# The mixer by pairs of sequences inside the first attention, with its short convolution's taps on ScalarE and VectorE

## The chip, the cores and the metric

The kernel runs on one core of a Trainium2 chip. The metric is the device time of one execution in microseconds (us). TensorE (PE in the rows) multiplies matrices, VectorE (DVE), ScalarE (ACT) and GpSimd (POOL) work on tiles of 128 partitions, and SyncE (SP) issues most DMAs. Each engine takes its own instructions strictly in order and waits on semaphores that the others raise.

## The reference

One decoder layer on 16 sequences of 128 tokens with 128 channels. The first stage, the mixer, is all that the change rewrites:

```python
x = jnp.einsum('bld,de->ble', u, W_in) + b_in          # 128 -> 3 * 128 channels
uc = dw_causal_conv(x, short_w, short_b)               # depthwise, 3 taps
q, k, v = uc[:, :D], uc[:, D:2 * D], uc[:, 2 * D:]
v = dw_causal_conv(k * v, inner_w, inner_b)            # depthwise, 4 taps
y = einsum('bld,de->ble', q * v, W_out) + b_out
x = layernorm(x_in + y)
```

Then come a self attention and a cross attention (16 heads of 64, each followed by a residual sum and a layer norm), a feed forward of width 512, and a last stage with 16 experts. The inputs are fp32; projections are made from a high and a low fp32r part of each factor, in three products (`mm_split`).

## The kernel before

`build` calls four things in a row: the allocations, `setup_and_mixer`, `attentions`, `feed_forward`. Each of the last three is a block of its own, so no engine starts on the attentions before all of them have left the mixer.

**The mixer** (`setup_and_mixer`, L162 to L497) works on groups of four sequences (512 columns), in ticks. The short convolution is folded into the weights: VectorE multiplies `w_in` with `tap_rows` (L379), ScalarE and VectorE split the result (L271, L382), and TensorE sums three shifted products for each of the three thirds of the channels (L476 to L478, nine products of 512 columns each). ScalarE adds the bias (L285), GpSimd corrects the first two columns (L333) and forms `KV` (L337), VectorE makes the inner convolution (L408, L412), GpSimd the gate (L342), TensorE the output product (L486), VectorE the residual and its statistics (L419 to L429), GpSimd the power (L353), ScalarE the normalised `N1` (L294), TensorE its transposes (L494), ScalarE and VectorE the parts of `x1T` (L300, L438), and GpSimd two sums for later residuals (L362). The same ticks split the six attention weights and the context (L306, L449, L313, L455) out of a ring of four raw tiles.

**The attentions** (`attentions`) are a software pipeline over 32 items, an item being one sequence in one of the two attentions. Iteration p of the loop does, on every engine, some part of items p-4 to p+1, in an order that is written out by hand. On TensorE: the value product `v_half`, four units of queries and keys `unit` (a pair of sequences is spread over two iterations), the transposes of the probabilities of item p-1, the output product `out_proj` of p-2, the scores of p+1, and the product with the values `p_v` of p-1. VectorE takes the maxima of the scores (L804, 16 heads in four quarters), reciprocals (L814), the copies of transposes (L830) and keys (L822), and the residual of p-2 (L839). ScalarE takes the exponentials (L729) and the copies of queries, values and outputs (L739, L748, L756), GpSimd the normalisation of the probabilities (L903). The scores of p+1 need the last copies of keys and transposes on VectorE; the transposes of an item need all the maxima of the next, as both use banks 2 and 3.

Of the kernel before, what the change touches and what calls it, by code (L numbers as in the profile page):

```python
# [22 lines left out]
F32 = mybir.dt.float32  # L23
# [9 lines left out]
FF = 512  # L33
NEXP = 16
RAW_SLOTS = 4
# [5 lines left out]
PAIR = 2  # L41
PCOLS = PAIR * L
# [8 lines left out]
FF_LOADS = 14  # L51
# [26 lines left out]
class Kernel:  # L78
    def __init__(self, nc, io):
        self.nc, self.io = nc, io  # L80

    def sb(self, ctx, name, shape, dt=F32):
        return ctx.enter_context(self.nc.sbuf_tensor(name, shape, dt))

    def split(self, ctx, name, shape):
        return Split(self.sb(ctx, name + "_hi", shape, F32R), self.sb(ctx, name + "_lo", shape, F32R))

# [7 lines left out]
def allocate(k, ctx):  # L95

    sb, split = k.sb, k.split
    k.ident = sb(ctx, "ident", [128, 128])
    k.half_neg = sb(ctx, "half_neg", [128, NSEQ])
    k.rows = {n: sb(ctx, "row_" + n, [128, 128]) for n in  # L100
              "sa_bo ca_bo ln1_g ln1_b ln2_g ln2_b fc2_b".split()}
    k.x1 = sb(ctx, "x1", [128, NSEQ, 128])
    k.xres = sb(ctx, "xres", [128, NSEQ, 128])
    k.x1T = split(ctx, "x1T", [128, T])


def allocate_attention(k, ctx):

    sb, split = k.sb, k.split
    k.maskb = sb(ctx, "maskb", [128, T], BF16)  # L110
    k.weights = {n: split(ctx, n, [128, INNER]) for n in WEIGHTS}
    k.wo_sa = sb(ctx, "wo_sa", [128, H // 2, 128])
    k.wo_ca = sb(ctx, "wo_ca", [128, H // 2, 128])
    k.ctxT = split(ctx, "ctxT", [128, T])


def allocate_feed_forward(k, ctx):

    sb = k.sb
    k.fc1 = k.split(ctx, "fc1", [128, FF])  # L120
# [6 lines left out]
    k.w1 = k.split(ctx, "w1s", [128, 128])  # L127
# [5 lines left out]
def load_feed_forward(k, sp, fc1_raw, w1_raw):  # L133

    nc, io = k.nc, k.io
    sp.dma_start(fc1_raw[:], io["fc1_w"]).then_inc(k.ff_ld, 16)
    sp.dma_start(w1_raw[:], io["W1_s"]).then_inc(k.ff_ld, 16)
    sp.dma_start(k.fc1_b[:], io["fc1_bT"]).then_inc(k.ff_ld, 16)
    sp.dma_start(k.fc2[:], io["fc2_w"].rearrange("(c p) n -> p c n", p=128)).then_inc(k.ff_ld, 16)
    row_broadcast(nc, sp, k.ln3_g[:], io["ln3_g"]).then_inc(k.ff_ld, 16)  # L140
    for tile, name in ((k.gainT, "g"), (k.shiftT, "b"), (k.b1_raw, "b1")):
# [11 lines left out]


def setup_and_mixer(k):

    nc, io = k.nc, k.io
    with ExitStack() as ctx:  # L162

        xT = k.split(ctx, "xT", [128, NSEQ, L + 2])
        zeros = k.sb(ctx, "zeros", [128, NSEQ, 2])
        xT_raw = k.x1
        c_raw = k.sb(ctx, "c_raw", [128, T])
        w_raw = k.sb(ctx, "w_raw", [128, RAW_SLOTS, INNER])
        w3_raw = k.sb(ctx, "w3_raw", [128, 3, 3 * D])
        w_in = k.sb(ctx, "w_in", [128, 3 * D])  # L170
        tap_rows = k.sb(ctx, "tap_rows", [128, 3, 3 * D])
        w3 = k.split(ctx, "w3", [128, 3, 3 * D])
        w_out = k.sb(ctx, "w_out", [128, D])
        mask_raw = k.sb(ctx, "mask_raw", [128, T], U8)
        taps = k.sb(ctx, "taps", [128, 3, 3])
        short_b = k.sb(ctx, "short_b", [128, 3])
        b_in = k.sb(ctx, "b_in", [128, 3])
        bias = k.sb(ctx, "conv_bias", [128, 3])
        early = k.sb(ctx, "early", [128, 3, 2])
        tap_b = k.sb(ctx, "tap_b", [128, 3, 3])  # L180
        inner = k.sb(ctx, "inner", [128, 4])
        inner_b = k.sb(ctx, "inner_b", [128, 1])
        b_out = k.sb(ctx, "b_out", [128, 128])
        ln3_b = k.sb(ctx, "ln3_b", [128, 128])
        C = k.sb(ctx, "C", [128, 2, 3, GRP, L])
        KV = k.sb(ctx, "KV", [128, GRP, L + 3])
        G = k.sb(ctx, "G", [128, GRP, L])
        yT = k.sb(ctx, "yT", [128, GRP, L])
        R = k.sb(ctx, "R", [128, GRP, 128])
        N1 = k.sb(ctx, "N1", [128, GRP, 128])  # L190
        stats = k.sb(ctx, "stats", [128, NSEQ, 6])
        mv = k.sb(ctx, "mv", [128, NSEQ, 2])
        rstd = k.sb(ctx, "rstd", [128, NSEQ])
        shift = k.sb(ctx, "mean_shift", [128, NSEQ])
        banks = k.banks(ctx, "mix")
        C_BANKS, OUT_BANK, XT_BANK = (0, 1, 2), 3, 4
        (ld_x0, ld_x, ld_win, ld_small, ld_tok, ld_rows, ld_keep, ld_ctx, ld_mask, ident0,
         ident_ok, zeros_ok,
         consts_ok, pads_ok, xhi, xlo, w3_ok, whi, wlo, raw_hi, kept_ok, tapb_ok, early_ok,
         bias_ok, w_hi, c_mm, c_ok, fix_ok, kv_ok, g_ok, y_ok, link, o_mm, r_ok, mv_ok, rstd_ok, shift_ok,  # L200
         n_ok, xT_mm, x1hi, x1lo, xb_ok, res_ok) = k.sems(ctx, "mix", """ld_x0 ld_x ld_win ld_small ld_tok
            ld_rows ld_keep ld_ctx ld_mask ident0 ident_ok zeros_ok
            consts_ok pads_ok xhi xlo w3_ok whi wlo raw_hi kept_ok tapb_ok early_ok bias_ok w_hi
            c_mm c_ok fix_ok kv_ok g_ok y_ok link o_mm r_ok mv_ok rstd_ok shift_ok n_ok xT_mm x1hi
            x1lo xb_ok res_ok""")
        ld_w = k.sems(ctx, "mix", " ".join("ld_" + n for n in WEIGHTS))
        ld_taps = k.sems(ctx, "mix", "ld_tap0 ld_tap1 ld_tap2")
        block = ctx.enter_context(nc.Block())
        ROWS = 1 + len(k.rows)
# [1128 lines left out]
```

## Time and profile before

| | |
|---|---|
| time, median of 3 runs | 546.56 us (544.33 to 548.43) |
| the profiled execution | 544.88 us, of which the span is 543.1 us |
| TensorE busy in the span | 475.7 us (88%) |
| VectorE, ScalarE, GpSimd busy | 393.5, 365.3, 257.3 us |
| first product of the attentions | 73.68 us after the span's start |
| first feed-forward work beside the last items | from about 478 us |

The span runs from the first to the last instruction. In a timeline row the first number is the start from the span's start, the second the duration, and the brackets say how long the engine had been idle and who ended that.

### The profile page before, as it was taken

How to read it: one execution, taken by the hardware profiler on the slowest of the kernel's cores; microseconds unless marked ns; L12 is line 12 of the kernel's file. 1: busy time of each engine (PE TensorE's matmuls, PEld its weight loads, DVE VectorE, ACT ScalarE, POOL GpSimd, SP SyncE). 2: the span in 40 equal slices, each digit the busy share in tenths (PEclk: the TensorE clock that was granted, in tenths of full speed). 3: DMA queues.
4: the chain of work that ended last, by engine and by line, in shares of the span. 5: the costliest groups of instructions: out<-in, count | busy, mean ns of one | idle time of the engine just before them, and what ended most of it. 6: DMA issues, size and time to landing. Idle time of an engine off the chain costs nothing. (4 is left out here: it accounts for less than half of the span.)

```text
span 543.1 us, 13796 instructions
## 1 busy us (share of the span) xinstructions
PE 475.7 (88%) x4554; PEld 434.5 (80%) x4554; DVE 393.5 (72%) x1846; ACT 365.3 (67%) x1374; POOL 257.3 (47%) x321
## 2 busy tenths in 40 slices
PE   3857267899999999999999999999999998989482
PEld 2646156799999999999999999999999987878372
DVE  3378835777878877787888778788777776368964
ACT  3165436888877888887787888768888867535534
POOL 0338823345445455544544554454455546333661
PEclk9969669999999999999999999999999999999666
DMA  6580020000000000000000000000000000040003
GB/s 208 167 292 2 0 59 3 2 2 2 3 2 1 2 1 2 2 2 2 1 4 2 2 2 2 3 2 1 2 1 2 3 2 2 1 161 2 2 18 78
DMA packets 14166, 14.22 MB, mean 26 GB/s; under 512 B 2832, under 2 KB 11152, under 8 KB 13968
## 3 DMA queue, kind: packets, MB, share of 16 engines
q1 hardware_dynamic: 13952, 13.08, 8.0%
q8 instruction: 37, 0.61, 0.5%
q14 instruction: 33, 0.27, 0.2%
q10 hardware_dynamic: 144, 0.26, 0.1%
HBM read 12.16 MB, written 1.18 MB: 25 GB/s over the span
## 5 line engine op out<-in xcount | busy, mean ns | idle before, releaser
L729 ACT ACTIVATE P<-P,at_negmax 128x128 f32<-128x128 f32 x512 | 198.8, 395 | 80.2 <-DVE at_negmax L804 80.2
L903 POOL TENSOR_TENSOR P<-P,at_inv 128x512 f32<-128x512 f32 x128 | 131.7, 1041 | 132.5 <-DVE at_inv L814 132.3
L804 DVE CUSTOM_DVE_ANT_0 P<-late_bank,maskb 128x128 f32<-128x128 f32 x512 | 110.7, 287 | 1.7 <-PE late_bank L660 1.7
L830 DVE COPY at_PT<-late_bank 128x512 f32<-128x512 f32 x128 | 87.9, 688 | 33.0 <-PE late_bank L643 32.7
L729 ACT ACTIVATION_READ_ACCUMULATOR P<-P,at_negmax 128x1 f32 x512 | 99.4, 194 | 0.0
L643 PE MATMUL late_bank<-ident,P 128*128 128x128 f32 x512 | 76.3, 272 | 2.6 <-issue 1.8
L660 PE MATMUL late_bank<-at_k,at_q 64*128 64x128 f32 x1024 | 65.8, 278 | 2.2 <-DVE at_k L822 2.2
L643 PEld LDWEIGHTS late_bank<-ident,P 128*128 128x128 f32 x512 | 59.4, 140 | 8.6 <-issue 4.4
L660 PEld LDWEIGHTS late_bank<-at_k,at_q 64*128 64x128 f32 x1024 | 59.7, 188 | 6.2 <-issue 2.7
L672 PE MATMUL late_bank<-at_PT,V 128*64 128x128 f32 x1024 | 63.0, 276 | 0.0
L672 PEld LDWEIGHTS late_bank<-at_PT,V 128*64 128x64 f32 x1024 | 55.2, 137 | 3.9
L822 DVE COPY at_k<-late_bank 128x512 f32<-128x512 f32 x64 | 44.2, 691 | 8.4 <-PE late_bank L75 7.4
L916 POOL TENSOR_TENSOR at_N<-at_N,row_ln_g 128x128 f32<-128x128 f32 x32 | 14.7, 460 | 65.3 <-DVE at_N L852 65.3
L804 DVE DVE_READ_ACCUMULATOR2_ANT at_negmax<- 128x1 f32 x512 | 42.7, 83 | 0.0
L739 ACT ACTIVATE at_q<-late_bank 128x512 f32<-128x512 f32 x64 | 37.6, 587 | 7.3 <-PE late_bank L75 7.3
L748 ACT ACTIVATE V<-late_bank 128x512 f32<-128x512 f32 x64 | 37.5, 586 | 0.0
L756 ACT ACTIVATE at_OT<-late_bank 128x512 f32<-128x512 f32 x64 | 34.1, 587 | 0.0
L839 DVE TENSOR_TENSOR at_R<-late_bank,xres 128x128 f32<-128x128 f32 x32 | 9.3, 292 | 33.4 <-PE late_bank L684 33.4
L814 DVE RECIPROCAL at_inv<-at_total 128x4 f32<-128x4 f32 x128 | 21.9, 172 | 15.9 <-ACT P L729 15.9
L684 PE MATMUL late_bank<-wo_sa,at_OT 128*128 128x128 f32 x256 | 31.2, 275 | 0.0
L684 PE MATMUL late_bank<-wo_ca,at_OT 128*128 128x128 f32 x256 | 31.2, 275 | 0.0
L476 PE MATMUL mix_bank<-xT_hi,w_hi 128*128 128x512 f32 x36 | 16.3, 454 | 16.5 <-DVE xT_lo L371 16.5
(182 smaller groups left out, 1074.0 us busy)
## 6 DMA issues: line engine op xcount, KB each, us to landing
c_raw<-in_ctxT SPq DMA_DIRECT2D x1, 1024.0 KB, 11.5
out<-xres SPq DMA_DIRECT2D x4, 224.0 KB, 2.5
x<-in_xT SPq DMA_DIRECT2D x1, 768.0 KB, 5.9
tap_rows<-in_short_wT SPq DMA_DIRECT2D x3, 192.0 KB, 5.7
w_raw<-in_sa_wq SPq DMA_DIRECT2D x1, 512.0 KB, 12.3
w_raw<-in_sa_wk SPq DMA_DIRECT2D x1, 512.0 KB, 13.1
w_raw<-in_sa_wv SPq DMA_DIRECT2D x1, 512.0 KB, 10.7
w_raw<-in_ca_wq SPq DMA_DIRECT2D x1, 512.0 KB, 10.5
```

Source lines behind the costliest of these rows:

```text
L643: last = nc.tensor.transpose(banks[T_BANK[g % 2]][:, h * 128:(h + 1) * 128], P[:, n % 2, HQ * g + h, :], k.ident[:])
L660: last = nc.tensor.matmul(score_bank(h), q[rows, t % 2, h // 2, pair], kk[rows, t % 2, h // 2, pair], start=True, stop=True)
L672: last = nc.tensor.matmul(banks[O_BANK[h // 8]][part:part + 64, h // 2 % 4 * 128:(h // 2 % 4 + 1) * 128], V[:, n % 2, h * DH:(h + 1) * DH] ...
L684: last = nc.tensor.matmul(banks[W_BANK][:, 0:128], OT[:, n % 2, c, :], out_w[att(n)][:, c, :], start=(c == 0), stop=(c == H // 2 - 1))
L729: last = nc.scalar.activation(P[:, n % 2, h, :], P[:, n % 2, h, :], ACT.Exp, scale=-1.0, bias=negmax[:, n % 2, h:h + 1], accum_out=total[: ...
L739: nc.scalar.activation(q[:, t % 2, u:u + 2, :], banks[UNIT_BANK[0]][:].rearrange("p (h l) -> p h l", h=2), ACT.Copy, scale=NEG_SCALE).then ...
L748: nc.scalar.activation(V[:, n % 2, half * 512:(half + 1) * 512], banks[V_BANK][:], ACT.Copy).then_inc(v_ok, 1)
L756: nc.scalar.activation(OT[:, n % 2, 4 * o:4 * o + 4, :], banks[O_BANK[o]][:].rearrange("p (c l) -> p c l", c=4), ACT.Copy).then_inc(ot_ok, 1)
L804: last = nc.vector.tensor_tensor_reduce(P[:, n % 2, h, :], score_bank(h), k.maskb[:, cols(n)], scale=1.0, scalar=3.0e38, op0=ALU.add, op1= ...
L822: nc.vector.tensor_copy(kk[:, t % 2, u - 1:u + 1, :], banks[UNIT_BANK[1]][:].rearrange("p (h l) -> p h l", h=2)).then_inc(k_ok, 1)
L830: nc.vector.tensor_copy(PT[:, HQ * g:HQ * g + HQ, :], banks[T_BANK[g % 2]][:].rearrange("p (h l) -> p h l", h=HQ)).then_inc(pt_ok, 1)
L903: nc.gpsimd.tensor_tensor(tile, tile, inv[:, n % 2, HQ * g:HQ * g + HQ].unsqueeze(2).to_broadcast([128, HQ, 128]), ALU.mult).then_inc(norm ...
```

## The change

`setup_and_mixer` and `attentions` become one function, `mixer_and_attentions`, with one loop from p = -7. The mixer works on pairs of sequences (256 columns). Pair m is projected in iteration 2m-6 (two thirds of the channels) and 2m-5 (the last third), goes through inner convolution, gate, output product and norm in 2m-4, and is transposed in 2m-3. Pairs 2 to 7 therefore have their convolution in iterations 0 to 10 and their transposes in 1 to 11, among the items of the first attention. The short convolution is no longer in the weights: TensorE makes one product of 256 columns for each third (three of `mm_split` instead of nine), ScalarE applies the tap without shift with its scale, and VectorE adds the two shifted taps from PSUM (`earlier_taps`), six instructions a pair. The splits of weights and context move too: the three of the self attention to iterations -4 and -3, the three of the cross attention to 1, 3, 5, the context's halves to 7 and 9. Raw tiles now lie where other tiles come later, `tap_rows` and its three DMAs are gone, and SyncE loads what the first pair needs first; `wo_ca` and the feed forward's tiles wait on SyncE until the last pair is done. The feed forward and all of the second attention keep their code.

```diff
+        PROJECT, CONVOLVE, TRANSPOSE = 6, 4, 3
+        C_BANK, X1T_BANK = (4, 5, 4), 5
...
+            def projection(p, m, c):
...
+                wait(pe, ot_ok, 2 * (p - 1))
+                wait(pe, tap_ok, (3 * m, 3 * m, 3 * m + 1)[c])
...
+                mm_split(nc, two(C_BANK[c]), w3, np.s_[:, c * D:(c + 1) * D], xT, np.s_[:, m % 2]).then_inc(c_mm, 1)
...
+                if p >= 0:
+                    mixer_output(p, pair_of(p, CONVOLVE))
                 unit(p, 2)
                 transposes(p - 1, 2)
+                projection(p, pair_of(p, PROJECT), 0)
+                projection(p, pair_of(p, PROJECT - 1), 2)
                 unit(p, 3)
                 transposes(p - 1, 3)
+                projection(p, pair_of(p, PROJECT), 1)
...
+                x1_transposes(p, pair_of(p, TRANSPOSE))
...
+                nc.scalar.activation(C[:, m % 2, c], two(C_BANK[c]), ACT.Identity, scale=taps[:, c, 2:3],
+                                     bias=bias[:, c:c + 1]).then_inc(c_ok, 1)
...
+                        nc.vector.scalar_tensor_tensor(out[:, :, back:], two(C_BANK[c])[:, :, 0:L - back],
+                                                       taps[:, c, j:j + 1], out[:, :, back:], ALU.mult,
+                                                       ALU.add).then_inc(tap_part if j else tap_ok, 1)
```

**ScalarE, from the second quarter's outputs of an even item to the middle of the next** (item 4; `P` the exponentials, `N1` the mixer's normalised pair, `at_OT` and `V` copies out of PSUM). Before:

```order
L756 ACTIVATE at_OT<-late_bank5 128x512
L739 ACTIVATE at_q<-late_bank0 128x512
L748 ACTIVATE V<-late_bank6 128x512
L729 ACTIVATE P,at_total<-P,at_negmax 128x128 x12
L764 ACTIVATE x1T_hi<-late_bank7 128x128
```

and after:

```order
L607 ACTIVATE at_OT<-late_bank5 128x512
L590 ACTIVATE at_q<-late_bank0 128x512
L599 ACTIVATE V<-late_bank6 128x512
L638 ACTIVATE C<-late_bank4,conv_bias,taps 128x256
L638 ACTIVATE C<-late_bank5,conv_bias,taps 128x256
L580 ACTIVATE P,at_total<-P,at_negmax 128x128 x4
L648 ACTIVATE N1<-R1,shift1,rstd1 128x128 x2
L580 ACTIVATE P,at_total<-P,at_negmax 128x128 x8
L615 ACTIVATE x1T_hi<-late_bank7 128x128
```

The run of twelve exponentials is split: the last four of item 4 come first, then `N1` of a pair, and only behind it the first eight of item 5.

**VectorE, in the middle of the same item** (`G` the inner convolution, `R1` the mixer's residual, `C` its channels). Before:

```order
L852 TENSOR_SCALAR at_N<-at_R,at_mv,at_rstd 128x128
L814 RECIPROCAL at_inv<-at_total 128x4 x2
L859 TENSOR_TENSOR x1T_lo<-late_bank7,x1T_hi 128x128
L830 COPY at_PT<-late_bank2 128x512
L822 COPY at_k<-late_bank1 128x512
```

and after, from its start and, behind the line of dots, from behind its last copy on:

```order
L774 TENSOR_SCALAR at_N<-at_R,at_mv,at_rstd 128x128
L838 TENSOR_SCALAR G<-KV,inner,inner_b 128x256
L842 SCALAR_TENSOR_TENSOR G<-KV,inner,G 128x256 x3
L733 RECIPROCAL at_inv<-at_total 128x4 x2
...
L858 BN_STATS stats1<-R1 128x6 x2
L862 BN_AGGR mv1<-stats1 128x2 x2
L865 TENSOR_SCALAR mv1<-mv1 128x2
L828 SCALAR_TENSOR_TENSOR C<-late_bank4,taps,C 128x2x127
L828 SCALAR_TENSOR_TENSOR C<-late_bank5,taps,C 128x2x127
L828 SCALAR_TENSOR_TENSOR C<-late_bank4,taps,C 128x2x126
L828 SCALAR_TENSOR_TENSOR C<-late_bank5,taps,C 128x2x126
L761 TENSOR_TENSOR at_R<-late_bank7,xres 128x128
```

Four instructions stand ahead of the reciprocals, and nine between the last copy and the residual of the attention.

**TensorE, in the second half of the next (odd) item** after the change; before it the unit of keys in bank 1 followed the transposes into bank 2 directly, and the output product the transposes into bank 3:

```order
L442 MATMUL late_bank2<-ident,P 128x128 x4
L73 MATMUL late_bank4<-xT_hi,w3_hi 128x256
L74 MATMUL late_bank4<-xT_lo,w3_hi 128x256
L75 MATMUL late_bank4<-xT_hi,w3_lo 128x256
L73 MATMUL late_bank1<-x1T_hi,sa_wk_hi 128x256
...
L442 MATMUL late_bank3<-ident,P 128x128 x4
L534 MATMUL late_bank5<-ident,N1 128x128 x2
L490 MATMUL late_bank7<-wo_sa,at_OT 128x128 x8
```

The projection of the last third stands ahead of the last unit, in bank 4, which `p_v` also uses and ScalarE's `at_OT` copy frees.

## Rows read from the trace of the kernel before

**Rows 1.** The page: granted clock in 40 slices; one group by line (busy, mean ns).
```profile
PEclk9969669999999999999999999999999999999666
...
L916 POOL TENSOR_TENSOR at_N<-at_N,row_ln_g 128x128 f32<-128x128 f32 x32 | 14.7, 460 | 65.3 <-DVE at_N L852 65.3
```

**Rows 2.** Busy time by stretch; columns: stretch, length, PE, PEld, DVE, ACT, POOL, clock.
```profile
0.00:73.66 73.66, 37.97 (x156) 29.96 (x157) 44.43 (x88) 29.41 (x50) 38.28 (x37) 0.82 0.39 123
114.49:209.50 95.01, 95.01 (x1017) 89.19 (x1017) 74.97 (x383) 74.38 (x311) 47.75 (x64) 1.00 0.01 2
```

**Rows 3.** Waits from 114.49 to 209.50 us: us in total, times, longest.
```profile
ACT P L729 <- DVE at_negmax L804: 20.7, 8, 2.7
DVE at_PT L830 <- PE late_bank L643: 8.5, 24, 0.4
DVE at_R L839 <- PE late_bank L684: 7.5, 8, 0.9
DVE at_inv L814 <- ACT P L729: 3.0, 8, 0.4
```

**Rows 4.** DMA issues: KB each, and us from issue to landing.
```profile
w_in<-in_W_in SPq DMA_DIRECT2D x1, 192.0 KB, 4.0
inner_b<-in_inner_b SPq DMA_DIRECT2D x1, 0.5 KB, 3.5
```

**Rows 5.** Timeline: a weight, then the attentions' start; VectorE L814 follows the maxima.
```profile
29.41 1.06 ACT L306 ACTIVATE sa_wq_hi<-w_raw 128x1024 fp32r<-128x1024 f32 x1 [10.92 <-DMA w_raw<-in_sa_wq]
...
73.68 0.55 PE L73 MATMUL late_bank<-x1T_hi,sa_wq_hi 128*128 128x256 f32 x1 [1.84 <-PEq L162]
...
87.87 0.17 DVE L814 RECIPROCAL at_inv<-at_total 128x4 f32<-128x4 f32 x1
...
97.13 0.17 DVE L814 RECIPROCAL at_inv<-at_total 128x4 f32<-128x4 f32 x1
...
107.14 0.17 DVE L814 RECIPROCAL at_inv<-at_total 128x4 f32<-128x4 f32 x1
```

**Rows 6.** Groups by line in the first 73.66 us: busy, mean ns of one.
```profile
L412 DVE SCALAR_TENSOR_TENSOR G<-KV,inner,G 128x512 f32<-128x512 f32 x12 | 9.0, 752 | 0.4
L285 ACT ACTIVATE C<-mix_bank,conv_bias 128x512 f32<-128x512 f32 x12 | 7.6, 677 | 3.0 <-PE mix_bank L478 3.0
L294 ACT ACTIVATE N<-R,mean_shift,rstd 128x128 f32<-128x128 f32 x16 | 6.6, 482 | 13.7 <-DVE mean_shift L433 13.7
L419 DVE TENSOR_TENSOR R<-mix_bank,xres 128x512 f32<-128x512 f32 x4 | 2.7, 686 | 3.7 <-POOL xres L347 3.7
L449 DVE TENSOR_TENSOR sa_wq_lo<-w_raw,sa_wq_hi 128x1024 fp32r<-128x1024 f32 x1 | 1.2, 1226 | 6.1 <-ACT sa_wq_hi L306 6.1
```

**Rows 7.** Timeline: work of VectorE beside work of GpSimd in the mixer.
```profile
46.42 0.68 DVE L438 TENSOR_TENSOR x1T_lo<-mix_bank,x1T_hi 128x512 fp32r<-128x512 f32 x1
46.44 1.29 POOL L362 TENSOR_TENSOR x<-N,ln_b 128x512 f32<-128x512 f32 x1
...
60.63 1.22 DVE L449 TENSOR_TENSOR ca_wv_lo<-w_raw,ca_wv_hi 128x1024 fp32r<-128x1024 f32 x1
60.72 2.25 POOL L342 TENSOR_TENSOR yT<-C,G 128x512 f32<-128x512 f32 x1 [1.57 <-DVE G L412]
...
61.76 2.29 DVE L455 TENSOR_TENSOR ctxT_lo<-c_raw,ctxT_hi 128x1024 fp32r<-128x1024 f32 x1
```

**Rows 8.** Timeline: one item of the first attention.
```profile
202.10 0.34 DVE L852 TENSOR_SCALAR at_N<-at_R,at_mv,at_rstd 128x128 f32<-128x128 f32 x1
...
206.28 1.04 POOL L903 TENSOR_TENSOR P<-P,at_inv 128x512 f32<-128x512 f32 x1 [0.23 <-DVE at_inv L814]
...
209.50 0.29 DVE L839 TENSOR_TENSOR at_R<-late_bank,xres 128x128 f32<-128x128 f32 x1 [0.94 <-PE late_bank L684]
...
211.69 0.55 POOL L910 TENSOR_TENSOR at_rstd<-at_mv,half_neg 128x1 f32<-128x1 f32 x1
211.97 0.39 ACT L729 ACTIVATE P<-P,at_negmax 128x128 f32<-128x128 f32 x1
```

More of the change, by code:

```diff
@@ L80, in __init__, with overlay @@
         self.nc, self.io = nc, io
+        self.taken = 0
+        self.raw = {}
+    def overlay(self, ctx, early, late):
+        start = self.taken
+        with ExitStack() as before:
+            early(self, before)
+        wanted, self.taken = self.taken - start, start
+        late(self, ctx)
+        spare = wanted - (self.taken - start)
+        if spare > 0:
+            self.sb(ctx, early.__name__ + "_rest", [128, spare], U8)
     def sb(self, ctx, name, shape, dt=F32):
+        size = {F32: 4, F32R: 4, BF16: 2, U8: 1}[dt]
+        self.taken += -(-size * int(np.prod(shape[1:])) // 32) * 32
         return ctx.enter_context(self.nc.sbuf_tensor(name, shape, dt))
@@ L561, in attentions @@
         rstd = k.sb(ctx, "at_rstd", [128, 1])
+        allocate_attention(k, ctx)
+        (w3, xT, w_out, b_out, taps, short_b, b_in, bias, edge, tap_b, inner, inner_b, C, KV, G, yT, R1, N1,
+         stats1, mv1, rstd1, shift1) = k.mixer_tiles
+        xT_raw, w_in = k.x1, k.w_in
         V, P, banks = k.V, k.P, k.late_banks
@@ L632, in v_half @@
                 wait(pe, v_ok, 2 * n + half)
+                if seq(n) == 0 and half == 0:
+                    wait(pe, w_lo, 3 * att(n) + 3)
                 mm_split(nc, banks[V_BANK][:], keys_T[att(n)], np.s_[:, cols(n)], values_w[att(n)],
@@ L682, in out_proj @@
                 wait(pe, r_ok, n)
+                if seq(n) == 0:
+                    pe.wait_ge(ld_wo, 16 * (att(n) + 1))
+                if pair_of(n + 2, CONVOLVE) is not None:
+                    wait(pe, r1_ok, pair_of(n + 2, CONVOLVE) + 1)
                 for c in range(H // 2):
@@ new lines, in mixer_normal, with x1_high @@
+            def mixer_normal(m):
+                if m is None:
+                    return
+                act.wait_ge(shift1_ok, m + 1)
+                wait(act, xT1_mm, m)
+                wait(act, res1_ok, 2 * m)
+                for b in range(PAIR):
+                    last = nc.scalar.activation(N1[:, b], R1[:, b], ACT.Identity, bias=shift1[:, b:b + 1],
+                                                scale=rstd1[:, b:b + 1])
+                last.then_inc(n1_ok, 1)
+            def x1_high(m):
+                if m is None:
+                    return
+                act.wait_ge(xT1_mm, m + 1)
+                nc.scalar.activation(k.x1T.hi[:, pcols(m)], banks[X1T_BANK][:, 0:PCOLS], ACT.Copy).then_inc(x1hi, 1)
@@ L868, in _ @@
+            first_weights()
+            x_low(1)
+            first_biases()
             for p in range(FIRST, ITEMS + 1):
```

725 lines of the change are left out of this document (389 added, 336 removed).

## The prediction

> **What bounds the kernel now.** The page's busy times (table above) are means over stages with different limits, so I went to the busy times by stretch [rows 2] and then to the waits of one stretch [rows 3]. Two stretches matter. In the first 73.66 us, the mixer, no engine is the bound: VectorE works 44.4 us of them, GpSimd 38.3, TensorE 38.0, ScalarE 29.4. They wait for each other and for loads, of which the late one is `sa_wq`: ScalarE idled 10.9 us for it and began at 29.41 [rows 5]. In the first attention (114.49 to 209.50 us, eight items) TensorE is busy for all of 95.01 us at clock 1.00. The residual on VectorE stands at 114.49 (where the stretch was cut) and again at 209.50, eight items later [rows 8], so an item costs 95.01 / 8 = 11.88 us, and it is TensorE's 11.88.
>
> The other engines have room, but not much. VectorE is busy 74.97 / 8 = 9.37 us an item. Its idle time, put down by the waits to transposes, output products and exponentials, is 8.5 + 7.5 + 3.0 = 19.0 us, or 2.4 an item [rows 3]. ScalarE waits 2.6 us an item, all at one place, ahead of the exponentials. Both rooms are smaller than what the change brings, and this is the question: how much of the 73.66 us comes back, and how much the items then lose.
>
> **What comes back.** I use as marker the end of the maxima of item 0, where VectorE's first reciprocal starts: 87.87 us [rows 5]. Everything after it is the old pipeline with additions.
>
> In the new kernel `w_in` is again the first load and took 4.0 us from its issue; the last of the five small loads that the bias needs took 3.5 [rows 4]. It is now issued near 4.5 us, as the tap rows ahead of it are gone; it lands at 8, and the bias needs 1 us of tiny VectorE work: 9.0. From there I lay pair 0 end to end. Prices for 256 columns come from the 512-column rows less the slope: a PSUM sum 0.42 us (0.686 for 512 at L419 [rows 6], 0.292 for 128 at L839 [rows 8]); a dependent two-operand step 0.48 (0.752 at L412). ScalarE (0.677 for 512 at L285 [rows 6], 0.4 for 256) twice and two rounds of taps for thirds 0 and 1, 3.35 with the waits between them; last third (product, ScalarE, two taps) 2.3; `KV` 1.0; inner convolution 2.0; gate and output product at the low clock 1.75; residual and statistics 1.4; then on VectorE the taps of pair 1 and the split of `sa_wq` (1.226, L449), 3.3; shift, two normalisations on ScalarE (0.48 each), transposes and two halves of `x1T` 2.9, less 1.35 of overlaps among them. Sum 16.65, so the first unit of the attentions can run at 25.65 instead of 73.68.
>
> Up to the marker VectorE leads again: the split of `sa_wv` and a low part 2.2, convolution of pair 1 1.9, a key copy 0.7, waiting for a cold unit, projection and output product 3.1, residual, key copy and statistics 2.0, taps 1.75, shift and mask 1.4, a late unit and its two key copies 2.7, taps 1.05, `x1T_lo` 0.4, sixteen maxima and a low part 4.3: 21.5. The marker falls at 47.1 instead of 87.87. **Gain: 40.8 us.** The bounds are 37 and 44, from the loads and the cold clock.
>
> **What the items lose.** Added to VectorE in an even item: inner convolution 0.42 + 3 x 0.48 = 1.9; residual 0.42; statistics 0.8; four taps 1.75; shift 0.15; together 5.0. In an odd item: two dependent taps 1.0, `x1T_lo` 0.42, the next `xT_lo` 0.42 and a split of 1.22: 3.1. No row shows a two-operand step with a PSUM operand; it lies between the 0.42 of the sum and the 0.48 of the dependent step, and I take 0.44. The folded-weight products leave TensorE, but its new work in a pair of items is still nine products of 256 columns, two of `w_out` and two transposes, 1.8 us. VectorE needs 2 x 9.37 + 8.1 = 26.8 us for a pair of items that took 23.76. It becomes the bound.
>
> Then the order. I walked a pair of items with these prices, from the last maximum of an even item at 0.
> - Even item. Normalisation, convolution and reciprocals end at 2.5 (before, 1.0). GpSimd's quarter (1.04 [rows 8]) and its gate end at 4.1, so the mixer's output product, wanted at 2.3, ends at 4.7; TensorE's room swallows that. Three pairs of copies end at 8.35, statistics and taps at 10.95, the attention's residual at 11.9. Eight maxima end at 13.7. `shift1` then waits for GpSimd: its last quarter 1.04, the attention's power 0.55 [rows 8] and the mixer's, some 0.7, all behind the reciprocal at 12.05: 14.4. Eight more maxima: 16.3.
> - Odd item. ScalarE is in order: `N1` stands ahead of the first exponentials. It ends at 15.5, and eight exponentials at 0.39 each [rows 8] end 2.3 us into the odd item, where they ended at 0.7. The next four end at 5.0, the copies of `at_OT` at 6.1. The last third's projection waits for these copies, since it shares bank 4, and the last unit stands behind it on TensorE: the last copy ends at 8.75, taps, `x1T_lo`, residual at 11.1, eight maxima at 12.95, `xT_lo` and the split at 15.3, eight maxima at 17.0.
>
> I take 16.1 and 16.5, as waits of this kind overlap a little: 32.6 for 23.76, +8.85 a pair of items. Four full pairs (items 2 to 9) give 35.4, less 0.5 as item 9 lacks `xT_lo`. Items 0 and 1 took 9.26 and 10.01 us (97.13 - 87.87, 107.14 - 97.13 [rows 5]) and I get 13.8 and 14.5: +9.0. Item 10 has no projection: +2.4; item 11 +1.2. **Loss: 47.5 us.** The lower bound is VectorE packed without a hole: 43.6 us of new work in twelve items less 12 x 2.4 of room, 14.8. The upper bound is 56.
>
> Splits of `ca_*` and the context are inside this sum. What leaves the mixer's block otherwise costs nothing later: `wo_ca` and the feed forward's loads are issued around item 11 and wanted at items 16 to 18, and the second attention keeps 11.88 or less.
>
> One resource cuts in. Where VectorE split a weight beside GpSimd's gate, GpSimd took 2.25 us instead of 1.29 and VectorE's next split 2.29 instead of 1.22; a VectorE sum out of PSUM beside GpSimd's 1.29 kept its 0.68 [rows 7]. So a step with both operands in SBUF and GpSimd's step exclude each other, and taps from PSUM are free of it. Half of this, 0.7 an odd item, is in my walk for the split.
>
> The Trainium skill, "GPSIMD Engine Reference", section "1. Specifications", says that GpSimd contends with VectorE instructions in a two-port mode or with two SBUF inputs. By that, the inner convolution's three steps (both operands in SBUF) would also take turns with the attention's three affine steps on GpSimd.
>
> **Sum.** 544.88 - 40.8 + 47.5 = 551.6 us. The profiled execution is 1.7 us under the median of 546.56, so this is 0.9% over that median.
>
> **Rivals.**
> - *VectorE packs well, faster.* Against my walk: a pair of items holds only 26.8 us of VectorE work, and of the 5.8 us of holes half hang on two places, `shift1` behind GpSimd and the bank 4 wait. If the holes shrink to 1 us a pair, a pair costs 27.8, +4.0: four pairs 16, the rest 8: 24. Time 544.9 - 40.8 + 24 = 528. For it: waits of 0.4 before a copy today are TensorE's pace [rows 3] and vanish when VectorE is late. Without holes at all it is 519. Halfway to my walk it is 540.
> - *Convolution against affine steps, slower.* Items 4, 6, 8, 10 have three GpSimd affine steps of 0.46 (L916 [rows 1] and two like it) just where the convolution runs. If they exclude each other, each such item loses up to 1.4 us, and the odd items the other half of their split's turn, 0.7: 4 x 1.4 + 5 x 0.7 = 9. Time 560. It decides from the point where the convolution's steps show more than 0.6 us. Against it: no row has these two side by side, so it may be less.
> - *The start gives less.* If the loads of `sa_wq`, `sa_wk` and `x` crowd as before (29.41 for the first [rows 5]), the first unit slips towards 32 us: time 558. Against it: by the order of the loads in the code some 5 MB stood ahead of `sa_wq` before (all of `x` twice, the context, the tap rows, eight rows of 64 KB), and about 1 MB does now.
> - *The clock falls.* In the mixer it stood at 0.82, among the items at 1.00 [rows 2]. TensorE would be busy some 80% of an item. The page's slices show 6 and 9 in the mixer and in the last stage alone [rows 1]; if it fell among the items, VectorE would still be the bound for most of it: +3.
>
> **How the numbers follow.** My walk holds, 546 to 559: 0.47, of which 0.24 stay under 552. VectorE packs well, under 541: 0.28. Between the two, 541 to 546: 0.08. Convolution against affine steps, or a late start, over 552: 0.15. The clock: 0.02. About 1% is what a measurement of this kernel can tell from no change, that is 541.1 to 552.0. Faster 0.28, same 0.33, slower 0.39. The range reaches down to the packed case's 528 and up to the 560 of the second rival; what is left out is 0.1 on either side.
>
> **What the changed kernel's profile would show.** The marker (the first reciprocal) at 47 us, the first unit near 26. Residuals in the first attention in turns of about 16.1 and 16.5 us up to item 11, then 11.9. ScalarE's wait for `shift1` in even items, some 4 us; VectorE's wait for exponentials in odd ones, 1.5. A step of `earlier_taps` at 0.5, `G` at 0.5 or, by the second rival, above 0.6. TensorE's busy time in items 2 to 9 near 80%. I am wrong if pairs of items take under 30 us or the marker is outside 44 to 51.

## The result, and the profile after

The changed kernel takes 558.68 us (median of 4 runs, 556.95 to 560.64) against 545.84 for the kernel before beside it: ratio 1.023, 95% interval 1.018 to 1.029. It is slower by more than the bound of 1%. I had forecast 551.6 with a range of 528 to 560, so the time lies in the range, 7.1 us above the number. The profiled execution has a span of 558.8 us against 543.1.

The page of the changed kernel, its busy times, its granted clock, and the groups that answer to the table shown of before:

```profile
PE 475.0 (85%) x4518; PEld 433.8 (78%) x4518; DVE 412.6 (74%) x1925; ACT 370.5 (66%) x1390; POOL 262.8 (47%) x348
...
PEclk9988899999979998999999999999999999997765
...
L970 POOL TENSOR_TENSOR at_N<-at_N,row_ln_g 128x128 f32<-128x128 f32 x32 | 15.2, 474 | 57.4 <-DVE at_N L774 57.4
...
L648 ACT ACTIVATE N<-R,shift,rstd 128x128 f32<-128x128 f32 x16 | 7.0, 487 | 36.0 <-DVE shift L871 36.0
```

Against [rows 1] there are a 7 and an 8 in the clock line in the middle of the first attention (slices 12 and 16), where all was 9, and ScalarE idles 36.0 us ahead of the mixer's normalisations, where it idled 13.7 us [rows 6].

The start, from the timeline of the changed kernel: the first unit of the attentions, and the end of the maxima of item 0, where the inner convolution follows in this kernel and not a reciprocal.

```profile
26.69 0.58 PE L73 MATMUL late_bank<-x1T_hi,sa_wq_hi 128*128 128x256 f32 x1 [1.13 <-DVE x1T_lo L878]
...
47.78 0.41 DVE L838 TENSOR_SCALAR G<-KV,inner,inner_b 128x256 f32<-128x256 f32 x1
```

These answer to 73.68 and 87.87 in [rows 5]. The gain at the start is 87.87 - 47.78 = 40.1 us.

What the items lose is read best from one last maximum of an item to the next, the way in which the walk of the prediction ran. Worked out from the timelines (the sixteenth maximum of each item ends at 47.87, 62.43, 77.51, 93.26, 109.94, 126.20, 143.02, 159.28, 178.26, 194.50, 210.45, 226.99, 240.19 in the changed kernel):

| item | before | forecast | after |
|---|---|---|---|
| 0, 1 | 9.26, 10.02 | 13.8, 14.5 | 14.56, 15.08 |
| 2, 3 | 11.83, 11.80 | 16.1, 16.5 | 15.75, 16.68 |
| 4, 5 | 11.89, 11.89 | 16.1, 16.5 | 16.26, 16.82 |
| 6, 7 | 11.89, 11.88 | 16.1, 16.5 | 16.26, 18.98 |
| 8, 9 | 11.89, 11.89 | 16.1, 16.0 | 16.24, 15.95 |
| 10, 11 | 11.88, 11.89 | 14.3, 13.1 | 16.54, 13.20 |

The twelve items take 192.3 us where they took 138.0: a loss of 54.3 against the 47.5 of the forecast. From item 12 on they take 11.9 again. The last stage, from the last residual (485.42; 471.00 before) to the end of the span, is 73.4 us against 72.1. So 54.3 - 40.1 + 1.3 = 15.5 of the 15.7 us; the other 0.2 us lie between the start of item 12 and the last residual.

Busy time of one pair of items (residual to residual, items 4 and 5), which answers to [rows 2], and VectorE's waits in it, which answer to [rows 3]:

```profile
120.86:153.95 33.09, 26.71 (x273) 24.22 (x273) 26.42 (x117) 22.65 (x86) 17.66 (x23) 1.00 0.01 2
```

```profile
DVE at_inv L733 <- ACT P L580: 1.9, 2, 1.4
DVE at_PT L749 <- PE late_bank L442: 1.6, 3, 0.7
DVE at_k L741 <- PE late_bank L75: 1.4, 2, 1.1
DVE shift L871 <- POOL rstd L1013: 0.7, 1, 0.7
DVE R L851 <- PE late_bank L523: 0.5, 1, 0.5
```

VectorE is busy for 26.4 us of 33.1 and waits at these five kinds of places for 6.1 of the other 6.7; I had counted 26.8 of work. TensorE, which was busy all the time, is now busy for 81%. No engine is full: the loss is made of work and of holes, and the experiments ask which holes can be closed and whether the work itself counts.

The rows behind the three largest holes, from the timeline of the changed kernel. First, the head of the odd item, VectorE and ScalarE:

```profile
124.30 0.16 DVE L871 SCALAR_TENSOR_TENSOR shift<-mv,rstd 128x2 f32<-128x2 f32 x1 [0.68 <-POOL rstd L1013]
...
124.50 0.88 ACT L648 ACTIVATE N<-R,shift,rstd 128x128 f32<-128x128 f32 x2 [4.38 <-DVE shift L871]
...
128.49 0.18 DVE L733 RECIPROCAL at_inv<-at_total 128x4 f32<-128x4 f32 x1 [1.36 <-ACT P L580]
```

Then the last unit of the odd item, behind the last third's projection, and the output product in the even item, TensorE and VectorE:

```profile
132.14 0.39 PE L73 MATMUL late_bank<-xT_hi,w_hi 128*128 128x256 f32 x1 [0.43 <-ACT at_OT L607]
...
133.50 0.69 DVE L741 COPY at_k<-late_bank 128x512 f32<-128x512 f32 x1 [1.06 <-PE late_bank L75]
...
147.36 0.71 PE L523 MATMUL late_bank<-w_out,yT 128*128 128x128 f32 x4 [1.73 <-POOL yT L998]
...
149.26 0.69 DVE L749 COPY at_PT<-late_bank 128x512 f32<-128x512 f32 x1 [0.73 <-PE late_bank L442]
```

### The profile page after: what moved, and what is told of

It is laid out like the page before. It is cut to its first block and busy times, and to the rows that moved or that the text cites. A ratio compares the mean times of both kernels' runs of the same rounds, so it can differ in the third digit from the quotient of the medians.

```text
span 558.8 us, 13934 instructions
## 1 busy us (share of the span) xinstructions
PE 475.0 (85%) x4518; PEld 433.8 (78%) x4518; DVE 412.6 (74%) x1925; ACT 370.5 (66%) x1390; POOL 262.8 (47%) x348
## 5 line engine op out<-in xcount | busy, mean ns | idle before, releaser
L749 DVE COPY at_PT<-late_bank 128x512 f32<-128x512 f32 x128 | 87.7, 687 | 33.3 <-PE late_bank L442 33.1
L442 PE MATMUL late_bank<-ident,P 128*128 128x128 f32 x512 | 78.9, 279 | 15.2 <-DVE at_negmax L723 13.3
L442 PEld LDWEIGHTS late_bank<-ident,P 128*128 128x128 f32 x512 | 60.9, 143 | 23.1 <-issue 18.9
L648 ACT ACTIVATE N<-R,shift,rstd 128x128 f32<-128x128 f32 x16 | 7.0, 487 | 36.0 <-DVE shift L871 36.0
L1381 POOL TENSOR_TENSOR ffrstd<-ffmv,half_neg 128x4 f32<-128x4 f32 x16 | 16.3, 1019 | 30.9 <-DVE ffmv L1274 30.9
## 6 DMA issues: line engine op xcount, KB each, us to landing
xres<-in_x SPq DMA_DIRECT2D x1, 768.0 KB, 12.3
```

What stands on the lines that cost most here:

```text
L442: last = nc.tensor.transpose(banks[T_BANK[g % 2]][:, h * 128:(h + 1) * 128], P[:, n % 2, HQ * g + h, :], k.ident[:])
L749: nc.vector.tensor_copy(PT[:, HQ * g:HQ * g + HQ, :], banks[T_BANK[g % 2]][:].rearrange("p (h l) -> p h l", h=HQ)).then_inc(pt_ok, 1)
```

## The experiments

Each kernel is the changed one with the edit shown. "Even interval" and "odd interval" are the times between VectorE's residuals (L761) in the middle of the first attention, where the granted clock is 1.00: odd the one that ends in an odd turn of the loop (15.08 in the changed kernel), even the one that ends in an even turn (18.01). Ratios are to the kernel before, beside it. The time is a median of 2 runs (output product later; four moves and the shift) to 10; the last three columns are from the one profiled execution of each kernel.

| kernel | us | ratio, 95% interval | odd | even | last residual |
|---|---|---|---|---|---|
| changed kernel | 558.7 | 1.023 (1.018, 1.029) | 15.08 | 18.01 | 485.42 |
| normalisations later | 547.1 | 1.003 (1.000, 1.005) | 13.39 | 17.98 | 473.64 |
| shift later too | 550.1 | 1.008 (1.005, 1.011) | 13.41 | 17.99 | 474.47 |
| no taps on VectorE | 547.1 | 1.003 (1.001, 1.005) | 15.08 | 16.94 | 472.70 |
| no taps, 27 products | 563.2 | 1.031 (1.026, 1.035) | 15.79 | 18.37 | 485.05 |
| last third later | 542.2 | 0.993 (0.990, 0.996) | 12.71 | 18.00 | 471.86 |
| output product later | 538.6 | 0.986 (0.979, 0.993) | 13.39 | 16.85 | 464.64 |
| splits moved | 549.1 | 1.005 (1.001, 1.008) | 14.53 | 16.55 | 475.22 |
| four moves together | 532.3 | 0.975 (0.970, 0.980) | 13.67 | 15.43 | 458.31 |
| mixer first | 576.3 | 1.057 (1.055, 1.059) | 11.91 | 12.43 | 502.67 |
| four moves and the shift | 535.4 | 0.982 (0.980, 0.985) | 13.68 | 15.39 | 461.63 |

**The mixer's normalisations behind the exponentials.**

```diff
                 exps(p, 0)
                 exps(p, 1)
+                mixer_normal(pair_of(p, TRANSPOSE))
...
-                mixer_normal(pair_of(p, CONVOLVE))
```

> Only the place of the mixer's normalisations on ScalarE changes: they stand behind the next item's first eight exponentials and not ahead of them. Holes theory: VectorE's loss in the pairs of items is its own work (26.4 us busy) plus some 6.5 us of holes, and the holes at the head of an odd item (0.49 + 1.36 us of wait for exponentials at 126.95 and 128.49 us) are caused by these normalisations, which wait 4.4 us for shift1. Then the odd items get 1.5 to 1.8 us shorter, six of them, and the time falls from 558.7 by 9 to 11 us, to about 549 (ratio to before near 1.005); the waits of at_inv for exponentials are under 0.3. Rival: the hole only moves (the next transposes, units or the mixer's transposes are late instead), and the time falls by under 3 us, to 556 or more.

The time fell by 11.5 us in the medians. The odd interval fell by 1.69 and the even one by 0.03 at most. VectorE's waits for exponentials over 86 to 236 us went from 9.2 us to 0.4 (this kernel, waits):

```profile
DVE at_inv L733 <- ACT P L580: 0.4, 1, 0.4
```

So 0.9 us of work, put in the wrong place of an in-order engine, cost 1.7 us in each pair; it did so because it waited there for 4.4 us and held the next item's exponentials up. Five odd intervals at 1.69 are 8.4 us, not 11.5. In the profiled executions, which are 15.0 us apart, another 2.1 are the fall of the clock in item 7, which this run does not have, and 3.2 are the last stage (70.2 us for 73.4), which the edit does not touch. So a part of the 11.5 is not the move's.

**VectorE's shift later as well.**

```diff
                 maxima(p, 3)
+                mixer_shift(pair_of(p, TRANSPOSE))
...
-                mixer_shift(pair_of(p, CONVOLVE))
```

> As the run with the normalisations later, and VectorE's mixer_shift also goes behind the last eight maxima of the next item. Holes theory: the wait of 0.68 us for GpSimd's power ahead of shift1 goes too, in seven items: 4 us less than with the normalisations alone, about 545 us, the time of the kernel before. Rival: shift1 comes 1.7 us later, so the x1 transposes come late and the hole is filled by waits further on: within 1.5 us of the other run.

The rival holds in the items: the wait of 0.68 us is gone and both intervals are the same to 0.03 us. The time missed both expectations, as it is 2.9 us above the other run and not within 1.5. Its timeline has the hole again, a little later:

```profile
123.88 0.18 DVE L733 RECIPROCAL at_inv<-at_total 128x4 f32<-128x4 f32 x1 [0.31 <-ACT P L580]
...
124.81 0.29 DVE L781 TENSOR_TENSOR x1T_lo<-late_bank,x1T_hi 128x128 fp32r<-128x128 f32 x1 [0.75 <-ACT x1T_hi L615]
```

With the normalisations alone, the second wait was 0.37 and the first was not there. ScalarE's exponentials are a second chain just behind VectorE's, so what VectorE arrives earlier it waits there. In the profiled executions this run is 4.1 us longer: its first residual comes 0.8 us later (87.47 for 86.71) and its last stage takes 3.2 us more (73.4 for 70.2); between the first and the last residual nothing changed.

**The taps left out, and the taps as products.** In the first, VectorE's `earlier_taps` is gone and ScalarE's copy releases the third. The second also issues TensorE's three products of a third three times, 27 for a pair of sequences in the place of 9. Neither computes the reference.

```diff
-                earlier_taps(pair_of(p, PROJECT), (0, 1))
-                earlier_taps(pair_of(p, PROJECT - 1), (2,))
...
+                for j in range(3):      # second kernel only
+                    for w, x in ((w3.hi, xT.hi), (w3.hi, xT.lo), (w3.lo, xT.hi)):
```

> Leaves out earlier_taps, the two steps for each third in which VectorE adds the two earlier taps; the last tap on ScalarE stays, so this computes less than the reference. It prices the second half of the change apart from the first. If VectorE is the bound as I said, its 1.64 us an even item and 0.99 us an odd item come back nearly in full in the ten items that have them (13 us), with some 4 to 6 us more at the start, where they stand in pair 0's chain: 540 to 543 us. Rival, order and not work sets the items (waits for GpSimd, ScalarE and transposes): VectorE then waits longer at the same places, the items give back under 5 us, and the time is 549 or more.

> Leaves out earlier_taps as well, and TensorE projects each third three times over, 27 products of 256 columns for a pair of sequences instead of 9, as folded taps would need (with the same weights each time, so the numbers are not the reference's). It stands for pairs in the attention with the taps left in the weights, without the cost of folding them. TensorE gets 18 x 0.107 = 1.9 us more in a pair of items in which it is busy for 26.7 of 33.1 us. If VectorE is the bound, this adds 0 to 3 us to the run without taps in the items, and some 3 us at the start where the clock is low: about 544 us. Rival: the added products stand ahead of the last unit and the last transposes, VectorE's copies wait for them in full: 1.9 x 5 + 3 = 12 us more than without taps.

Without its taps VectorE is busy for 24.5 us of a pair instead of 26.4 to 26.7, and the pair gives 1.07 back (32.02 for 33.09), all in the even interval. What the odd interval saved became a wait for TensorE:

```profile
129.11 0.29 DVE L761 TENSOR_TENSOR at_R<-late_bank,xres 128x128 f32<-128x128 f32 x1 [0.82 <-PE late_bank L490]
```

Another 5.8 us come from the start (first residual at 82.14 for 87.93), where the taps stand in the chain of pair 0 as expected. The total, 11.6 us, lies between the two expectations. Between the first and the last residual this kernel is 6.9 us shorter in the profiled executions, but 3.8 of these are the intervals of items 7 and 10 (15.06 for 17.23, 15.76 for 17.35), where the changed kernel's clock fell and this one's did not; the missing taps themselves are worth some 3 us there. So in the items the order set most of the pace, not VectorE's work. The products showed the same from the other side. TensorE's busy time in a pair rose by 2.1 us (products that follow each other start 0.117 us apart, and not the 0.107 of the expectation) and the pair by 2.15 (34.17 for 32.02), although TensorE was busy only 83 to 84% of it: the products stand ahead of units and transposes for which VectorE waits. My theory's "0 to 3 us" for them was wrong, the rival was right. So the second half of the change is not what made the kernel slower: taps on VectorE cost 11.6 us by the medians, and six more products a third cost 16.1 by the medians (12.3 in the profiled executions) in this schedule, even before any folding of weights.

**The last third's projection later, and the output product later**, each on top of the normalisations' move:

```diff
-                projection(p, pair_of(p, PROJECT - 1), 2)
                 unit(p, 3)
                 transposes(p - 1, 3)
+                projection(p, pair_of(p, PROJECT - 1), 2)
```

```diff
-                mixer_output(p, pair_of(p, CONVOLVE))
                 unit(p, 2)
                 transposes(p - 1, 2)
+                mixer_output(p, pair_of(p, CONVOLVE))
```

The third moves only among the items, and with the output product VectorE's `mixer_residual` goes behind its next copy.

> The kernel with the normalisations later (its odd interval between residuals was 13.39 us, its even one 17.98), and among the items TensorE's projection of the last third stands behind the last unit and the last transposes, where it stood ahead of them. Holes theory: VectorE's wait of 1.06 us for the last unit's key product in the odd interval goes nearly away, as the unit no longer waits 0.43 us for at_OT nor for three products: the odd interval is 12.4 to 12.6, the even one stays, and the last residual comes 4 to 5 us earlier. Rival: the taps of the last third wait instead, since TensorE and ScalarE must bring that third behind the transposes: the odd interval stays within 0.3 us of 13.39.

> The kernel with the normalisations later, and in even items TensorE's mixer output product stands behind the third unit and the third transposes, and VectorE's mixer_residual one copy later. Theory: the even interval of 18.0 us, which did not move when VectorE got 0.68 us less to wait for elsewhere, holds 1.58 us of VectorE's waits (0.49, 0.73, 0.37) that all come from TensorE's wait of 1.7 us for GpSimd's gate. The even interval becomes 16.4 to 16.7 and the odd one stays at 13.4: 8 to 9 us in six items. Rival: the residual then waits for the product instead and statistics and taps behind it slip: the even interval stays above 17.5.

The last third gave 0.68 us in the odd interval (I had wanted 0.8 to 1.0) and nothing in the even one; the last residual came 1.8 us earlier, not 4 to 5. The output product gave 1.13 in the even one (wanted 1.3 to 1.6), nothing in the odd one, and 2.7 in the last interval with a mixer's output (14.61 for 17.31), that of item 10, one of the two large misses of my table. Of these 2.7 us only some 1.1 are the hole; the rest is the clock, as the account of item 10 below shows. Each hole belongs to one interval, and closing it moves only that one. The whole second move is worth 9.0 us at the last residual, the clock of item 10 included.

**The splits where GpSimd is idle**, on top of the normalisations' move: `weight_low` and `context_low` two items later, ahead of `x1_low` and the residual.

```diff
+                if p in (3, 5, 7):
+                    weight_low(CA[p // 2 - 1])
+                elif p in (9, 11):
+                    context_low((p - 9) // 2)
                 x1_low(pair_of(p, TRANSPOSE))
```

> The kernel with the normalisations later, and the low parts of the three cross-attention weights and of the context are made two items later, just ahead of VectorE's residual, where GpSimd waits for the next reciprocals and is idle. Nothing else moves. Contention theory: such a split took 1.75 to 1.76 us where it ran beside GpSimd against 1.22 alone, and x's low part 0.67 against 0.41; the split goes back to 1.22 and the intervals of a pair, 31.37 us together, get 0.5 to 0.7 shorter, 3 us in five pairs. Rival: the split delays the residual and with it GpSimd and TensorE, or GpSimd's later work meets another of VectorE's steps: no change of the pair within 0.3 us.

The contention is real and worth little. In the changed kernel, VectorE and GpSimd side by side, against this kernel's split with GpSimd idle:

```profile
105.65 0.93 DVE L794 TENSOR_TENSOR xT_lo<-x,xT_hi 128x256 fp32r<-128x256 f32 x1
106.50 1.76 DVE L883 TENSOR_TENSOR ca_wk_lo<-ca_wk_raw,ca_wk_hi 128x1024 fp32r<-128x1024 f32 x1
...
106.25 0.92 POOL L1023 TENSOR_TENSOR x<-N,row_ln_b 128x256 f32<-128x256 f32 x1
107.13 1.19 POOL L987 TENSOR_TENSOR C<-C,edge 128x12 f32<-128x12 f32 x1
```

```profile
130.36 1.22 DVE L883 TENSOR_TENSOR ca_wk_lo<-ca_wk_raw,ca_wk_hi 128x1024 fp32r<-128x1024 f32 x1
```

The split is back at 1.22, but the pair is only 0.29 shorter (14.53 + 16.55 = 31.08 for 31.37), the rival's case, and VectorE now reaches its next steps beside GpSimd (last section). Two of this kernel's even intervals are 18.11 and 17.86 and not 16.55; the granted clock was 0.91 and 0.90 in them and 1.00 in the short one. These 2.9 us and a last stage of 72.1 us for 70.2 are more than the 3.5 us by which its profiled execution is the longer one, so its time says nothing of the move.

**The four moves together.**

> All four moves together (normalisations, last third, output product, splits), the work unchanged. If the loss is holes of the order, they add up: 547.1 - 4.5 - 8.5 - 3 = 531 us, a pair of items near 28 us against VectorE's 26.2 busy, ratio to before 0.973. Rival: TensorE or the chain of one item (maxima, exponentials, GpSimd, transposes) is the next bound, and the parts do not add: 537 or more.

532.3 us, 2.5% under the kernel before and 26.4 us under the changed kernel, with the same work. I had expected 531 from the parts. The intervals add up: the four moves by themselves took 1.69, 0.68, 1.13 and 0.29 us off a pair, 3.79 together, and all four took 3.99 (29.10 for 33.09). The pair from 115.98 to 145.23 us (last maxima, items 5 and 6) and VectorE's waits in it:

```profile
115.98:145.23 29.25, 26.44 (x269) 24.23 (x269) 25.98 (x118) 22.62 (x87) 16.63 (x23) 1.00 0.01 2
```

```profile
DVE at_PT L752 <- PE late_bank L442: 0.8, 2, 0.5
DVE shift L874 <- POOL rstd L1016: 0.7, 1, 0.7
DVE at_k L744 <- PE late_bank L75: 0.6, 1, 0.6
DVE x1T_lo L784 <- ACT x1T_hi L618: 0.4, 1, 0.4
DVE P L726 <- issue: 0.2, 1, 0.2
```

VectorE is busy 89% of the pair now, against 80%, and TensorE 90%, against 81%. The twelve items take 165.9 us (47.32 to 213.18), 27.9 more than before.

> All four moves and mixer_shift behind the last maxima as well. With the normalisations alone this move took VectorE's wait of 0.68 us away and gave nothing, because VectorE then waited 0.38 us longer for the low part of x1T and 0.31 for the exponentials. If ScalarE's sixteen exponentials are the next bound of the odd interval (they are ScalarE's and start with the maxima), this does not change with the other moves: the odd interval stays within 0.1 us of 13.67. Rival: the wait was hidden by the late units and thirds and comes out now: 13.0 and 530 us or less.

With the shift later as well the odd interval is 13.68 for 13.67, so this hole stays hidden behind ScalarE's chain in the better order too. The run is 3.1 us longer, all of it ahead of the first residual (85.07 for 81.63).

**The mixer ahead of the attentions, in the new code.**

```diff
-        FIRST, FIRST_UNITS = -7, -2
+        FIRST, FIRST_UNITS = -21, -2
-        PROJECT, CONVOLVE, TRANSPOSE = 6, 4, 3
+        PROJECT, CONVOLVE, TRANSPOSE = 20, 18, 17
...
-                if p % 2 and p >= -3:
+                if p % 2 and p >= 3 - PROJECT:
```

> The changed kernel with the mixer's pairs of sequences all ahead of the attentions: the same code, loads and taps, but each pair is projected, convolved and transposed 14 turns earlier, so that nothing of it stands between the attention's instructions. It undoes the first half of the change and keeps the second. Between the taps of pair 1 (21.07) and of pair 2 (35.34) VectorE took 14.3 us, of which three weight splits, the mask and three key copies are some 5: one pair alone takes 9 to 10 us, seven more than one pair before the first unit. Theory: the 40 us at the start come from the overlap with the items and not from the loads or the taps. Then the last maximum of item 0 falls at 47.9 + 6.5 x 9.5 = about 108 us, items are 11.9 again, and the time is 560 to 572. Rival: the 40 us come mostly from the new order of the loads and from one projection in the place of nine products, so that the last maximum of item 0 still falls before 80 us and the time is under 540.

576.3 us. Stretches of this kernel, the first from the first pair's `x1T_lo` to the last pair's, the second the twelve items:

```profile
24.70:103.00 78.30, 29.64 (x100) 21.84 (x101) 47.32 (x130) 21.83 (x48) 32.85 (x50) 1.00 0.08 31
116.52:257.44 140.92, 135.63 (x1430) 125.64 (x1430) 111.18 (x564) 114.65 (x466) 66.39 (x85) 1.00 0.01 2
```

A pair by itself takes 78.3 / 7 = 11.2 us (I had 9.5), with the busiest engine at 60%; so my time for this kernel was too low, but the theory holds and the rival (the 40 us come from loads and fewer products) falls. It gives an account of the first half of the change, with the loads, the splits of weights and the taps where they are. The last maximum of item 0 falls at 116.52 with the mixer first and at 47.87 with the pairs inside: the overlap saves 68.7 us. The items then take 192.3 instead of 140.9: it costs 51.4. The net, 17.2, less the 1.3 us by which the last stage is shorter, is the 15.9 between the two profiled spans; the medians are 17.6 apart. Against the kernel before, the small pairs and the taps on VectorE would have cost 116.5 - 88.0 = 28.6 us at the start if they were not overlapped; the old mixer worked on four sequences at a time. In all the change buys 68.7 us and pays 28.6 of them back at the start and some 54 in the items.

## Why the prediction came out as it did

- **Gain at the start**: 40.8 forecast, 40.1 measured; the bias was ready at 9.2 us (9.0), the first unit ran at 26.69 (25.65), the marker fell at 47.8 (47.1). Right, and the mixer-first run shows that its cause is the overlap.
- **Mechanism of the loss**: right by its rows. ScalarE waits 4.4 us for `shift1` (some 4 forecast), VectorE 1.4 for exponentials (1.5), bank 4's wait for `at_OT` is there (0.43), and TensorE is at 81% (some 80). Moving `N1` and the last third away showed both causes to be worth 1.7 and 0.7 us a pair.
- **Size of the loss**: 54.3 for 47.5, that is 6.8 us: the clock in items 7 and 10 (3.8), items 0 and 1 (1.3), my shading of the walk (0.9), the rest of item 10 (0.6), and 0.1 in item 11. The walk gave 16.3 and 17.0; items 4 to 6 measured 16.26, 16.82, 16.26. Then I wrote that waits of this kind "overlap a little" and took 16.1 and 16.5. They did not overlap: in the runs each hole stands in its own interval and moves no other. This shading cost about 0.9 us over items 2 to 9, apart from the clock, as item 2 was 0.35 shorter than taken. Items 0 and 1 took 1.3 more than I gave them; their clock was 0.88 and 0.89 (rows below), and how much of the 1.3 is the clock no run sets apart.
- **The clock**: I gave it a chance of 0.02 and 3 us. It is the largest single part of what the forecast was short (7.1 us of time, 9.0 of span). The step that failed is that TensorE at 80% would keep 1.00 (a term of nothing in the sum). Item 7 took 18.98 where item 5, its counterpart one pair earlier at 1.00, took 16.82: 2.2 us. Item 10 took 16.54; in the kernel without taps, which does the same work in this item, as no pair is projected any more, it took 14.89 at 1.00: 1.7 us. Stretches of items 0, 1 and 10 of the changed kernel, then of item 10 without taps and with the output product moved (columns as in [rows 2], then the shares of the DMA):

```profile
47.87:62.43 14.56, 9.21 (x66) 7.80 (x66) 9.76 (x53) 8.15 (x31) 5.42 (x6) 0.88 0.00 0
62.43:77.51 15.08, 12.49 (x115) 11.18 (x115) 11.13 (x49) 13.95 (x58) 8.30 (x9) 0.89 0.01 2
210.45:226.99 16.54, 14.27 (x131) 13.25 (x131) 12.93 (x60) 7.06 (x28) 8.13 (x11) 0.90 0.01 2
...
199.31:214.20 14.89, 12.62 (x131) 11.66 (x131) 12.77 (x61) 6.99 (x28) 8.12 (x11) 1.00 0.01 2
...
193.98:207.77 13.79, 12.86 (x131) 11.69 (x131) 12.62 (x60) 8.62 (x38) 8.12 (x11) 1.00 0.01 2
```

- **Item 10**: 14.3 forecast, 16.54 measured. Of the 2.2 us 1.7 are the clock. For the rest a step of the walk failed, "TensorE's room swallows that", of the output product that waits for the gate: TensorE waited 2.1 us for `yT`, and at the full clock moving the product takes 14.89 to 13.79 here, 1.1 us, as in each other even item (1.13). The walk's total for even items was right although this step in it was not, so another of its terms was too large; which one I can't say.
- **The last stage** took 1.3 us more, at a mean clock of 0.74 for 0.78. Whether the one is from the other is not shown: the kernels without taps and 27 products, and with the splits moved, ran it in 72.0 and 72.1 us at 0.76 and 0.75.
- **VectorE packs well** (528) did not happen in this order. It nearly did in another: the four moves gave 532.3. In a pair it reached 29.1 us where the rival had 27.8. The rival was a statement on the schedule, and I treated it as a matter of chance. By the rows I could have listed the holes by the engine that makes each, as the run of the four moves does.
- **Convolution against affine steps** (560): the number is near, the mechanism is not the cause. The three two-operand steps beside three GpSimd steps took 1.77 us for 1.53 alone, 0.57 for each in the trace where the rival needed more than 0.6, and the first step kept its 0.40. That is 0.24 us an even item and not 1.4. The split's turn (1.76 for 1.22) and that of `xT_lo` (0.67 or 0.93 for 0.42) together are near the 0.7 that the walk took.
- **Of the sum**: 543.1 - 40.8 + 47.5 = 549.8 of span was forecast and 558.8 measured: 0.7 of gain, 6.8 of items, 1.3 of the last stage, and 0.2 from item 12 to the last residual. All four went the same way. That the time still lies in the range is in part luck: 558.7 is at the very end of the 546 to 559 that I gave to the walk, and the 560 at which the range ends came from the rival with the affine steps, which had no part in it.

What stays open: why the granted clock falls after some pauses and not after others like them, and why the last stage, which no edit touched, took between 70.2 and 73.4 us over the kernels. No run here sets that apart, and it is as large as several of the differences between medians above; the intervals between residuals at a clock of 1.00 are free of it.

## What to carry to other kernels

Work that is put into the gaps of a full pipeline should be followed on every in-order engine it touches: here one pair of normalisations on ScalarE and one output product on TensorE, neither on the engine that leads, cost 1.7 and 1.1 us a pair of items, more together than all the taps on VectorE (1.07), and four moves of instructions with no work removed turned +2.3% into -2.5%. List the holes by the engine that makes each and by the interval in which they stand; such holes add up, while a hole with a second chain close behind it (the shift) gives nothing. A size taken from a step-by-step walk should be kept as the walk gives it, and a stretch in which TensorE will no longer be busy all the time needs a term for the clock.

## What the runs showed of the hardware

**The clock falls inside a busy stretch after short pauses.** Windows of the changed kernel in item 7 and in item 10; the column before the last two is the clock, of which 0.50 is the 1.2 GHz level:

```profile
160.00:162.00 2.00, 0.76 (x7) 0.56 (x5) 0.61 (x4) 2.00 (x11) 1.84 (x4) 0.90 0.00 0
162.00:168.00 6.00, 5.77 (x24) 5.37 (x25) 2.69 (x6) 4.70 (x15) 2.18 (x3) 0.50 0.01 1
212.00:216.00 4.00, 1.88 (x14) 1.50 (x13) 3.45 (x11) 1.14 (x4) 3.47 (x5) 1.00 0.00 0
216.00:222.00 6.00, 6.00 (x44) 5.88 (x44) 3.61 (x11) 2.62 (x10) 1.12 (x2) 0.72 0.02 4
```

TensorE was busy 0.76 of 2 us, or 1.88 of 4, before it fell. The same two pauses in items 3, 5 and 9 (1.0 to 1.1 us, then 1.3 to 1.5) brought no fall. In item 10 TensorE waits 2.1 us for the gate in seven kernels (2.4 in the one with the splits moved): in six of them the clock of the stretch from 200 to 220 us is then 0.91, in the one without taps it stays at 1.00. In the three kernels with that product moved the wait is 0.3 us and the clock of this stretch is 1.00. So a hole can cost twice, as a wait and as slower products behind it (1.1 and 1.7 us in item 10), but it does not always.

**GpSimd and VectorE take turns for some forms only.** In the kernel with the four moves, `at_N` and the first convolution step (one tensor operand each, in SBUF) stand beside GpSimd's two-operand steps of 256 columns:

```profile
158.28 0.75 DVE L777 TENSOR_SCALAR at_N<-at_R,at_mv,at_rstd 128x128 f32<-128x128 f32 x1
158.98 0.81 DVE L841 TENSOR_SCALAR G<-KV,inner,inner_b 128x256 f32<-128x256 f32 x1
...
158.22 0.72 POOL L994 TENSOR_TENSOR KV<-C 128x256 f32<-128x256 f32 x1
158.90 0.74 POOL L1008 TENSOR_TENSOR xres<-xres,b_out 128x256 f32<-128x256 f32 x1
```

They took 0.75 and 0.81 where they took 0.34 and 0.40 in the changed kernel (142.94 and 143.20 us), while GpSimd's steps kept their length. Both ended just after the GpSimd step that had begun before them. Who begins first matters: at 143.20 us the convolution step began 0.16 us ahead of a GpSimd step and kept its 0.40. The two-operand steps of the convolution, with both operands in SBUF, lost 0.08 each, though GpSimd had begun first. So here the one-operand form was held up until GpSimd's step had ended, and the two-operand form of the convolution hardly.

The Trainium skill, "GPSIMD Engine Reference", section "1. Specifications", says that GpSimd contends with VectorE instructions in a two-port mode and with those that have two SBUF inputs. Of the second kind the subtractions of the splits agree (1.76 for 1.22), and the convolution's scalar-tensor-tensor steps show next to nothing (0.56 for 0.48). Whether `at_N` and the first convolution step are of the first kind no row says.
